# Seven chained stages on one core: linear attention in another order, and stage ends without GpSimd's drain and clear

## The reference

```python
x = _layernorm(x + _L0_attn_ref(x, ...))            # causal attention, latent projections
x = _layernorm(x + _L0_xattn_ref(x, ctx, ctx, ...)) # strided cross attention
x = _layernorm(x + _L0_ffn_ref(x, ...))             # 64 experts, 6 a token, and a shared one
x = _layernorm(x + _L1_attn_ref(x, ...))            # linear attention
x = _layernorm(x + _L1_xattn_ref(x, ctx, ...))      # cross attention with a gate
x = _layernorm(x + _L1_ffn_ref(x, ...))             # FFN with ternary weights
```

```python
sink_incoming    = 1.0 / einsum('nhld,nhd->nhl', q + EPS, k.sum(axis=2) + EPS)
source_outgoing  = 1.0 / einsum('nhld,nhd->nhl', k + EPS, q.sum(axis=2) + EPS)
conserved_sink   = einsum('nhld,nhd->nhl', q + EPS, (k * source_outgoing[..., None]).sum(axis=2) + EPS)
conserved_source = einsum('nhld,nhd->nhl', k + EPS, (q * sink_incoming[..., None]).sum(axis=2) + EPS)
conserved_source = clip(conserved_source, -1.0, 1.0)
sink_allocation    = sigmoid(conserved_sink)
source_competition = softmax(conserved_source, axis=-1) * s
kv  = einsum('nhld,nhlm->nhdm', k, v * source_competition[..., None])
out = einsum('nhld,nhdm->nhlm', q * sink_incoming[..., None], kv) * sink_allocation[..., None]
return out @ Wo.T + bo
```

## Time and profile before

| | |
|---|---|
| median of 3 runs | 2148.85 us (2148.22 to 2149.18) |
| the profiled execution | 2143.36 us |
| its span in the trace | 2141.6 us |
| PE, DVE, ACT, POOL busy | 86%, 65%, 47%, 47% |
| mean granted TensorE clock | 0.90 |
| stage ends (SP released behind the second barrier) | 317.4, 510.9, 738.6, 923.4, 1196.5, 1950.8, 2141.5 us |

### The profile page before, as it was taken

How to read it: one execution, slowest core, us unless ns; L and a number is a source line. 1 busy time by engine, 2 the same in 40 slices (tenths; PEclk the granted TensorE clock), 3 DMA queues, 4 the chain that set the end, 5 groups by cost and what they waited for, 6 DMA issues and landing times. The chain is left out here.

```text
span 2141.6 us, 61119 instructions
## 1 busy us (share of the span) xinstructions
PE 1847.7 (86%) x21583; PEld 1364.0 (64%) x21586; DVE 1385.0 (65%) x3373; ACT 1013.2 (47%) x2025; POOL 1008.6 (47%) x1077
## 2 busy tenths in 40 slices
PE   6999979997999399936888599999999999984675
PEld 3777758886888277725666367676667676752333
DVE  4777755775877544423555457676777777755998
ACT  2555533442111034424666255555555555534997
POOL 1333331221777524356773255656565656541433
PEclk9999998997999599968999799999999999985555
DMA  6311118992221299743331110101010010000111
GB/s 197 99 36 34 34 41 286 330 330 99 62 54 52 69 297 269 221 116 96 116 118 34 51 34 27 38 26 36 28 33 31 30 34 28 19 11 29 59 59 42
DMA packets 157246, 192.98 MB, mean 90 GB/s; under 512 B 27987, under 2 KB 140758, under 8 KB 157157
## 3 DMA queue, kind: packets, MB, share of 16 engines
q1 hardware_dynamic: 146885, 189.20, 28.1%
q0 software_dynamic: 10272, 2.62, 0.6%
HBM read 140.91 MB, written 77.51 MB: 102 GB/s over the span
## 5 line engine op out<-in xcount | busy, mean ns | idle before, releaser
L3013 DVE TENSOR_REDUCE xa_kq<-xa_A 100x4 f32<-100x1444 f32 x128 | 212.6, 1661 | 157.9 <-PE xa_A L2682 157.9
L2841 ACT ACTIVATE xa_prob<-xa_A 121x1600 f32<-121x1600 f32 x96 | 144.5, 1505 | 234.1 <-PE xa_A L2709 234.1
L2916 POOL TENSOR_TENSOR xa_prob<-xa_prob,xa_exp_bias 121x1600 f32<-121x1600 f32 x64 | 228.7, 3574 | 41.1 <-ACT xa_prob L2841 41.0
L1430 POOL DMA_INDIRECT slot_rows<-rt_x_again,rt_slot_u x150 | 154.6, 1030 | 67.2 <-issue 62.3
L2941 POOL TENSOR_TENSOR xa_o_rstd<-xa_o_var,xa_power 100x1 f32<-100x1 f32 x32 | 17.8, 556 | 240.3 <-DVE xa_o_var L3053 240.3
L2709 PEld LDWEIGHTS xa_A<-xa_q2T,xa_kqT 17*121 17x121 f32 x3072 | 92.3, 184 | 46.7 <-issue 29.5
L1676 POOL DMA_INDIRECT contrib<-ex_y,ex_place_u x64 | 62.3, 974 | 120.6 <-ACT ex_y L1728 108.1
L2682 PE MATMUL xa_A<-xa_kqT 16*100 16x361 f32 x1024 | 112.5, 509 | 6.8 <-ACT xa_prob L2841 6.8
L2709 PE MATMUL xa_A<-xa_q2T,xa_kqT 17*121 17x100 f32 x3072 | 108.5, 278 | 4.8 <-DVE xa_kq L3013 4.2
L2626 PE MATMUL xa_C<-xa_wk,xa_rows_T 128*121 128x256 f32 x384 | 103.0, 406 | 1.7 <-ACT xa_rows_T L2821 1.7
L2626 PE MATMUL xa_C<-xa_wv,xa_rows_T 128*121 128x256 f32 x384 | 101.3, 401 | 0.0
(11 more groups left out here) (355 smaller groups left out, 4975.7 us busy)
## 6 DMA issues: line engine op xcount, KB each, us to landing
ex_w<-in_w13T SPq DMA_DIRECT2D x64, 352.0 KB
contrib<-xs_zero SPq DMA_DIRECT2D x30, 640.0 KB
la_rows<-contrib SPq DMA_DIRECT2D x16, 1200.0 KB
xs_ctxT<-in_ctxT SPq DMA_DIRECT2D x32, 512.0 KB
xa_rows_t<-in_ctx SPq DMA_DIRECT2D x96, 121.0 KB
ex_w<-in_w2T SPq DMA_DIRECT2D x64, 176.0 KB
slot_rows<-xs_zero SPq DMA_DIRECT2D x32, 272.0 KB
ex_x_t<-slot_rows SPq DMA_DIRECT2D x64, 136.0 KB, 6.9
```

The source lines that it names most:

```text
L1430: nc.gpsimd.indirect_dma_start(slot_rows, bass.IndirectOffsetOnAxis(slot_u[:, k, n:n + 1], 0), x_again[:, k, :], None, bounds_check=SLOTS ...
L2841: nc.scalar.activation(prob[:, n, :].rearrange("p (h a) -> p h a", h=HPG), A[:ROWS, :, 0:G * T], ACT.Exp, scale=EXP_SCALE).then_inc(exp_re ...
L2916: nc.gpsimd.tensor_tensor(chunk, chunk, exp_bias[:, n, :].unsqueeze(1).to_broadcast([ROWS, HEADS, T]), ALU.mult).then_inc(biased, 1)
L3013: nc.vector.tensor_reduce(kq[:T, k, NCH, 4 * j:4 * j + 4, DH:DH + 1].rearrange("p h o -> p (h o)"), A[:T, :, 0:src_len], axis=AXIS_X, op=A ...
```

## The change

Three things change. Stage ends: a block no longer ends with GpSimd's DRAIN; the semaphores of a stage are neither cleared nor followed by a second barrier there, but POOL clears them in the next stage, behind its first memsets, and once more at the end of the program, with a barrier. The linear attention, PE, DVE and ACT: the output projections run directly behind the denominators, and DVE's moments, aggregates and residual directly behind the reciprocal; ACT's allocate comes before the second half of the gates. The linear attention, POOL: `keep` runs before the last sums.

```diff
 class Store:
+    spent = []
...
     def end(self):
-        self.nc.clear_and_free_semaphores(self.semaphores)
-        self.nc.all_engine_barrier()
+        Store.spent = Store.spent + self.semaphores
+
+    @classmethod
+    def clear_spent(cls, nc):
+        nc.clear_and_free_semaphores(cls.spent)
+        cls.spent = []
...
-        with nc.Block() as block:
+        with nc.Block(no_gpsimd_drain=True) as block:
...
                 pool.wait_ge(power_set, 1)
+                Store.clear_spent(nc)
...
 # linear attention, POOL
                 def body(b, has):
-                    if b[1] < 2 and (has(2) or has(-3)):
+                    of = slice(0, 1 if b[1] == FIRST else 2)
+                    if has(3) and b[1] >= 2:
+                        add_halves(later(b, 3), of)
+                    if has(2) or has(-3):
                         roots(b, has)
+                    if has(0):
+                        keep(b)
                     if has(3):
-                        of = slice(0, 1 if b[1] == FIRST else 2)
-                        add_halves(later(b, 3), of)
+                        if b[1] < 2:
+                            add_halves(later(b, 3), of)
                         add_rows(later(b, 3), of)
-                    if b[1] >= 2 and (has(2) or has(-3)):
-                        roots(b, has)
-                    if has(0):
-                        keep(b)
...
 # linear attention, PE
                     if now:
                         denominators(b)
-                    if coming:
-                        project(later(b, 1), 0)
+                    if has(-2):
+                        project_out(later(b, -2), 0)
+                        project_out(later(b, -2), 1)
                     if prev:
                         keys_values(later(b, -1))
                     if now:
                         turn_inverse(b)
                     if coming:
-                        project(later(b, 1), 1)
+                        project(later(b, 1), 0)
...
                     if now:
                         turn_shares(b)
-                    if has(-2):
-                        project_out(later(b, -2), 0)
-                        project_out(later(b, -2), 1)
...
 # linear attention, ACT
                     if has(0):
                         sums_out(b)
+                        allocate(b)
                     if has(1):
                         gates(later(b, 1), 1)
-                    if has(0):
-                        allocate(b)
-                    if has(1):
                         gates_e(later(b, 1))
...
 # linear attention, DVE
                     if has(0):
                         invert(b)
+                    if has(2) or has(-3):
+                        moments(b, has)
+                        aggregate(b, has)
+                    if has(-2):
+                        residual(later(b, -2))
                     if has(-1):
                         mask_kv(later(b, -1))
                     if has(0):
                         bias_values(b)
                         second_weights(b)
-                    if has(2) or has(-3):
-                        moments(b, has)
-                    if has(0):
                         clip(b)
-                    if has(2) or has(-3):
-                        aggregate(b, has)
...
-                    if has(-2):
-                        residual(later(b, -2))
...
 # the end of the program
+    Store.clear_spent(nc)
+    nc.all_engine_barrier()
```

More of the change, by code:

```diff
@@ L1985, in body @@
                 def body(b, has):
-                    if b[1] < 2 and (has(2) or has(-3)):
-                        roots(b, has)
-                    if has(3):
-                        of = slice(0, 1 if b[1] == FIRST else 2)
+                    of = slice(0, 1 if b[1] == FIRST else 2)
+                    if has(3) and b[1] >= 2:
                         add_halves(later(b, 3), of)
-                        add_rows(later(b, 3), of)
-                    if b[1] >= 2 and (has(2) or has(-3)):
+                    if has(2) or has(-3):
                         roots(b, has)
@@ L1995, in body @@
                         keep(b)
+                    if has(3):
+                        if b[1] < 2:
+                            add_halves(later(b, 3), of)
+                        add_rows(later(b, 3), of)
                 periods(pool, NU, FIRST, LAST, REACH, body, 4)
@@ L2157, in body @@
                     if coming:
-                        project(later(b, 1), 2)
+                        project(later(b, 1), 1)
                     if now:
@@ L2161, in body @@
                     if coming:
-                        project(later(b, 1), 3)
+                        project(later(b, 1), 2)
                     if now:
                         conserved(b)
+                    if coming:
+                        project(later(b, 1), 3)
                     if prev:
```

## The result

The changed kernel takes 2137.82 us (median of 6 runs, 2129.81 to 2142.01), the kernel before 2148.53 in the same comparison (6 runs, 2145.43 to 2150.52). The ratio is 0.9964, 95% interval 0.9948 to 0.9980: 7.7 us faster, between 4.3 and 11.2. The two medians lie 10.7 us apart, which is inside this interval; in what follows a difference is that of the ratio. The forecast was 2139.0, and 9.9 less than before.

What follows compares the result with a forecast made beforehand. It took the changed places to be bound by waits: the slowest engine at stage-end barriers, and a ring across engines in linear attention. Terms: −8.8 − 3.6 + 2.5 = −9.9 us, forecast 2139.0, range 2131 to 2149.

Steps and rivals of the forecast that it cites:

- GpSimd's DRAIN, −8.8: Ends of routing and experts: the DRAINs of 3.5 and 5.3 us go entirely; bounds 0 and −8.8.
- Rival A: The DRAINs' time comes back as a wait in the next stage: 2147.7 us; chance 0.12.
- Clear and second barrier, −3.6: Six inner stage ends save 0.7 us each (−4.2), less small DRAIN and closing-clear costs; bounds −4.2 and −2.5.
- The start, −13.5: Linear attention's first units: POOL's keep-first order removes 7.4-us waits, unit 4 starts 13.5 us sooner; bounds −12 and −15.
- The moments' charge of 3.1: Unit 0 of linear attention: own_sums comes 3.1 us later, behind DVE's moments, which wait for POOL's sum.
- Rival C: The linear attention's start wins only half, as moments or new waits hold it: 2145.7 us; chance 0.13.
- The steady units, +9.5: Linear attention, units 4 to 14: residual waits for la_x_o, period 14.6 against 13.65, ten of them +9.5 us.
- Rival D: The residual's wait doesn't bind in linear attention: period 12.9, whole kernel 2117 us; chance 0.06.
- rival B: TensorE falls to 1.2 GHz in linear attention's new gap, 2.6 us a unit: 2168 or 2160 us; chance 0.09.
- PEclk full there: Sign of being right: TensorE's granted clock stays full in linear attention's steady units, with periods of 14.6 us.
- The last units, +6.5: End of linear attention: unit 14 costs +1.9 us, and what follows unit 15's den +4.6.
- the tail's +4.6: Linear attention after unit 15's den: own_sums at 7.0 instead of 2.9 us, and keys_values +0.5 behind a projection.

Runs made afterwards that it cites:

- e6: The kernel before with blocks that end without GpSimd's drain, clear and second barrier kept at each stage end: 2137.36 us, ratio 0.9960.
- e7: The kernel before with GpSimd's drain kept and the clears moved into the next stage, no second barrier: 2135.83 us, ratio 0.9951.
- e3: The changed kernel with PE, DVE and ACT in their old orders (stage ends and GpSimd's order alone): 2112.10 us, ratio to the kernel before 0.9834.
- e2: The kernel before with the linear attention's new orders alone, on all four engines, and the old stage ends: 2152.86 us, ratio 1.0036.
- e8: The changed kernel with one more all-engine barrier between cross attention and FFN: ratio to the kernel before 0.9967.
- e1: The kernel before with the changed kernel's stage ends alone (no GpSimd drain, clears in the next stage): 2129.94 us, ratio 0.9930.
- e5: The kernel of e3 with output projections between conserved sums and attend, residual between compete and weigh_values: 2097.82 us, ratio to the kernel before 0.9773.
- e4: The changed kernel with ACT's finish (la_x_o of b-4) ahead of inverse_out: 2116.20 us, ratio to the kernel before 0.9867.

## Why the prediction was right, by its steps

**GpSimd's DRAIN, −8.8.** Right in mechanism and size: e6 gives −8.6 alone (−5.4 to −11.8), and the exits follow POOL's branch by 0.3 us. Rival A is out.

**Clear and second barrier, −3.6.** Too small. The six barriers took 4.4 in the profile, as their rows said. The 0.35 charged for the other engines' DRAINs had no row and doesn't show: SP is released 0.2 us after its DRAIN starts in both kernels. The clear in the FFN has five ranges and not three, but the four behind the first take some 0.04 us each, and it is over at 1948.5, ahead of POOL's work at 1949.88. What was missed is the FFN's clock, −2.5. e7's −10.5 has some 4 more, for which the stages of its profile give no place; 6.9 is just outside its interval (7.1 to 13.9), so this part is open.

**The start, −13.5.** Right, and somewhat small. (The sum has a slip of 0.2: 981.8 + 27.2 is 1009.0.) Measured −14.6 from the stage's entry to unit 4's reciprocal (100.2 and 85.6); against the other profiles of the old order (101.6 to 103.4) it is −16 to −18. The moments' charge of 3.1 is what e3, without it, gets at unit 1 (44.1 us from entry to den against 47.3). Rival C is out.

**The steady units, +9.5.** The step was right in each time that it named: DVE waits for la_x_o (1.98), residual T + 5.15, own_sums T + 6.95, period 14.65 where 14.6 was forecast. Ten units came to +12.8 (148.8 against 135.9 between the reciprocals of units 4 and 14): 10.0 by the period, 2.5 by two units in which the clock fell, and the rest is rounding. Rival D, a shorter period, is out. The 2.5 are rival B in small, and "PEclk full there" was wrong: the granted clock over the stretch is 0.98, the fall costs 1.25 a unit and not the 2.6 worked out, since it lasts for a few instructions behind the gap, and it came in two of ten units here and three in e2. In e8, whose linear attention is the changed kernel's, it came in none, though each of its ten units has the same gap of 1.57 to 1.63 us on PE. In which units it falls is chance as far as these runs go. The Trainium skill's page "TensorE: Matmul & The Clock Gate", section "HAM oscillation — how this bites in real kernels", tells of a kernel in which every tile starts cold, behind waits for DMA that are longer than this gap. The prediction took it to say that this change pays in every unit; that is more than the page says, and the traces show two, three and no units of ten.

**The last units, +6.5.** Measured +1.5 for unit 14 and +6.7 from unit 15's reciprocal to the release: +8.2. In the tail's +4.6 one term was far too small, the 0.5 for keys_values behind a projection that waits for yT. Before, keys_values followed yT's copy at once:

```profile
1180.72 0.50 ACT L2267 ACTIVATE la_yT<-la_X 128x400 f32<-128x400 f32 x1 [3.53 <-PE la_X L2128]
...
1181.37 0.46 PE L2081 MATMUL la_X<-la_v,la_tok 100*32 100x32 f32 x32 [0.69 <-ACT la_yT L2267]
```

Now a whole projection stands between:

```profile
1176.55 3.40 PE L2149 MATMUL la_X<-la_wo,la_yT 128*100 128x256 f32 x8 [0.59 <-ACT la_yT L2278]
...
1179.87 0.46 PE L2092 MATMUL la_X<-la_v,la_tok 100*32 100x32 f32 x32
...
1179.98 0.69 DVE L2421 TENSOR_TENSOR la_r<-la_X,la_x_bo 100x512 f32<-100x512 f32 x1 [4.07 <-PE la_X L2149]
```

YT's copy starts at 1175.99, so it is 3.9 us from there to keys_values, where it was 0.65: +3.2. Of this 1.4 is the clock, since the projection takes 3.40 instead of 1.97 at 1.2 GHz; the mean clock from unit 15's conserved sums on is 0.72, and was 0.85. The other term, own_sums 4.1 later, measured 3.75.

**The sum.** The linear attention was forecast at +2.5 and came to +6.5 in the profile and +7.7 in e2; the ends at −12.4 and came to −15.0 in e1. The two errors are of like size and opposite, so that the total is nearer than its terms is luck.

## What to carry to other kernels

An instruction moved ahead in one queue brings all its waits along, second-hand ones too: ask for each wait where its signaller stands in its own queue, and what that one waits for. Here a residual with two buffers waited for a normalisation that stood behind an inverse that stood behind the moved projections, and swapping two instructions on a third engine was worth 21 us. An engine's order is best searched from both sides: the residual was too late in one kernel (la_x_bo held la_x) and too early in the other, and the place in between was worth 13 us more (e5 against e3).

## What the runs showed of the hardware

GpSimd's DRAIN at the end of a block that had issued indirect DMAs took 3.5 and 5.3 us though all their semaphores had been waited for, and 0.29 to 0.66 at the other five ends; without it, the DRAIN of the clear some 0.1 us later took 0.1 us (e6). In the profiles, TensorE's granted clock in the FFN was 0.53 in the three kernels with a semaphore clear and a barrier ahead of the FFN (before, e2, e6), and 0.67 to 0.68 in the eight others; the reason is open. A gap of 1.6 us on TensorE in each of ten units let its clock fall for a few instructions in two (the changed kernel), three (e2) or none (e8) of them; with no such gap (e4, e5) it didn't fall in the steady part.
